# Ends of the expert layers on ScalarE and VectorE alone, and A_log's exponential moved into the projection

## The chip, the cores and the metric

The kernel runs on 1 core of one Trainium2 chip. The metric is the device time of one execution in microseconds (us), and the number compared is the median over several executions.

## What is computed

The input is x, 4 sequences of 512 tokens with 256 channels (2048 rows). Four layers follow, each as x = x + layer(layernorm(x)): attention, an expert layer, a state-space layer, and the same expert layer again.

```
def _L0_ffn_ref(x, W1, b1, W2, b2, W3, b3, Wg, bg):
    gate_weights = softmax(x @ Wg + bg)
    topv, topi = top_k(gate_weights, 2)
    h = gelu(x @ W1[n] + b1[n]); h = gelu(h @ W2[n] + b2[n]); eo = h @ W3[n] + b3[n]
    out = sum over the two chosen experts of topv * eo
...
# state-space layer
dt = softplus(dt + dt_bias)
dA = exp(dt * (-exp(A_log)))
```

Each token thus ends an expert layer with three terms: its own row of x, gate 0 times the output row of its first expert, and gate 1 times that of its second.

## The kernel before, in words

The program is a row of stages, each a block in which all engines run their own instruction stream, with a barrier at its end: constants, layer norm, attention, `ffn_stage` (first expert layer), layer norm "ln2" (`layer_norm_stage`), `ssm_project_stage`, the heads of the state-space layer, `ffn_stage` again. X, [128 partitions, 16 token tiles, 256], stays in SBUF throughout. G is 4 groups of TB = 4 token tiles.

In `ffn_stage` tokens are sorted by expert, gathered in tiles of rows, put through three products with two gelus, and each output row is scattered by GpSimd to `y_rows` in DRAM. When all scatters have landed, the end of the layer begins: SP issues eight loads of 512 KB (L1018), one for each k (0: first expert's rows, 1: second's) and group g, into the tile `back`, in the order of the list BACK: (1,2), (0,0), (1,3), (1,0), (0,1), (1,1), (0,2), (0,3). Each has a semaphore of its own.

- For groups 2 and 3 (BY_POOL) ScalarE multiplies the second rows by their gates in place, four activations a group (L1261), and GpSimd adds the scaled group to X in one tensor_tensor of 128x1024 (L1076).
- VectorE does the rest: for each (k, g) left in that order, four scalar_tensor_tensor of 128x256 (L1449) that multiply a tile's rows by their gate and add them to X, 24 in all. Before the first rows of groups 2 and 3 it waits for GpSimd's sum.
- In the second expert layer only, ScalarE then issues the four stores of the output, 512 KB each (L1267), behind its own scaling in its stream, each when `added` shows that its group is complete.

In ln2, `SsmWeights` runs alongside: SP loads A_log into a_log (L1546) and other small inputs; behind the last activation of the stage ScalarE takes the exponential of a_log (L1565), for which a program puts an activation-table load ahead of it, and VectorE multiplies it by -1 into neg_a (L1560).

`ssm_project_stage` begins with TensorE's products for dt. ScalarE copies them with a bias (L1742, twice), then takes Abs (L1744), Exp (L1746) and Relu (L1747) of 128x1024, and only then the first taps of the convolution (L1755, from PSUM). VectorE adds three more taps to each (L1857, three instructions a block), which frees the bank for TensorE's third block after and lets ScalarE go on to Silu (L1769, with a table load). Between blocks VectorE does the steps of softplus (L1868, L1871, L1874). neg_a is first read much later, by an Exp at L1825.

Of the kernel before, what the change touches and what calls it, by code (L numbers as in the profile page):

```python
# [17 lines left out]
P = 128  # L18
# [858 lines left out]
def ffn_stage(nc, stage, ins, X, split_w, xn_rows, y_rows, row_moves, c, out, split_in):  # L877
# [9 lines left out]
    with ExitStack() as ctx:  # L887
# [63 lines left out]
        weighed, summed = sem("weighed"), sem("summed")  # L951
# [11 lines left out]
        BY_POOL = (2, 3)  # L963
        BACK = [(1, 2), (0, 0), (1, 3), (1, 0), (0, 1), (1, 1), (0, 2), (0, 3)]
# [56 lines left out]
        def _(pool):  # L1021
# [51 lines left out]
            for at, g in enumerate(BY_POOL):  # L1073
                pool.wait_ge(weighed, at + 1)
                x = X[:, g * TB:(g + 1) * TB, :]
                pool.tensor_tensor(x, x, back[:, G + g, :, :], ALU.add).then_inc(summed, 1)  # L1076
# [115 lines left out]
        def _(act):  # L1192
# [65 lines left out]
            for g in BY_POOL:  # L1258
                act.wait_ge(back_loaded[G + g], 16)
                for n in range(TB):  # L1260
                    ins_ = act.activation(back[:, G + g, n, :], back[:, G + g, n, :], ACT.Copy,  # L1261
                                          scale=gate[:, 1, g * TB + n:g * TB + n + 1])
                ins_.then_inc(weighed, 1)
            if out is not None:
                for g in range(G):
                    act.wait_ge(added, (2, 4, 5, 6)[g] * TB)
                    act.dma_start(group_rows(out.rearrange("b s d -> (b s) d"), g),  # L1267
                                  X[:, g * TB:(g + 1) * TB, :]).then_inc(stored, 16)
                act.wait_ge(stored, 16 * G)

        @block.vector
        def _(dve):
# [167 lines left out]

            order = [(k, g) for k, g in BACK if k == 0 or g not in BY_POOL]
            for at, (k, g) in enumerate(order):
                dve.wait_ge(back_loaded[k * G + g], 16)
                if g in BY_POOL:
                    dve.wait_ge(summed, BY_POOL.index(g) + 1)
                elif k:
                    dve.wait_ge(added, TB * (order.index((0, g)) + 1))
                for n in range(TB):
                    dve.scalar_tensor_tensor(X[:, g * TB + n, :], back[:, k * G + g, n, :], gate[:, k, g * TB + n:g * TB + n + 1],  # L1449
                                             X[:, g * TB + n, :], ALU.mult, ALU.add).then_inc(added, 1)  # L1450

# [76 lines left out]
class SsmWeights:  # L1528
# [6 lines left out]
    def __init__(self, t, ins, split, wih, wil, conv_w, conv_b, dt_bias, neg_a, d_col):  # L1535
        self.ins, self.split, self.wih, self.wil, self.conv_w, self.conv_b = ins, split, wih, wil, conv_w, conv_b
        self.dt_bias, self.neg_a, self.d_col = dt_bias, neg_a, d_col
        self.a_log = t.sb("a_log", [P, 1])
        self.loaded, self.exp_ready = t.sem("loaded"), t.sem("exp_ready")

    def sync(self, sp):
        ins, loaded = self.ins, self.loaded
        col = lambda name: ins["L0_attn_b_" + name].unsqueeze(1)
        for half in range(2):
            rows = slice(half * SH, (half + 1) * SH)
            sp.dma_start(self.a_log[rows, :], col("A_log")).then_inc(loaded, 16)  # L1546
# [10 lines left out]
    def vector(self, dve, g):  # L1557
        if g == 4:
            dve.wait_ge(self.exp_ready, 1)
            dve.tensor_scalar(self.neg_a[:, :], self.a_log[:, :], -1.0, None, ALU.mult)  # L1560

    def scalar(self, act, g):
        if g == 4:
            act.wait_ge(self.loaded, 9 * 16)
            act.activation(self.a_log[:, :], self.a_log[:, :], ACT.Exp).then_inc(self.exp_ready, 1)  # L1565
# [5 lines left out]
def ssm_project_stage(nc, XTh, XTl, weights, outs, identf, b_rows):  # L1571
# [9 lines left out]
    with ExitStack() as ctx:  # L1581
# [16 lines left out]
        names = ("cleared dt_psum dt_read dt_exp dt_u dt_done da_done ft_done suffix_done steps hi_done lo_done "  # L1598
# [140 lines left out]
        def _(act):  # L1739
# [6 lines left out]
            act.activation(e, e, ACT.Exp, scale=-1.0).then_inc(s["dt_exp"], 1)  # L1746
            act.activation(u, u, ACT.Relu).then_inc(s["dt_u"], 1)  # L1747
# [52 lines left out]
            for N in range(NB):  # L1800
# [22 lines left out]
                if (b, n) == (2, 0):  # L1823
                    act.wait_ge(s["dt_done"], 1)
                    act.activation(dA, dT, ACT.Exp, scale=neg_a[:, :]).then_inc(s["da_done"], 1)  # L1825
# [19 lines left out]
        def _(dve):  # L1845
# [19 lines left out]
            def softplus():  # L1865

                dve.wait_ge(s["dt_exp"], 2)
                steps(dve.tensor_scalar(dT, e, LOG_SERIES[-1], None, ALU.mult))  # L1868
# [634 lines left out]
```

## Time and profile before

| | |
|---|---|
| median of 3 runs | 1444.76 us (1443.35 to 1449.8) |
| the profiled execution's own time | 1445.6 us |
| its span in the trace | 1443.9 us |
| mean granted TensorE clock | 0.913 |
| PE busy | 1168.8 us (81%) |
| VectorE (DVE) busy | 989.5 us (69%) |
| ScalarE (ACT) busy | 641.4 us (44%) |
| GpSimd (POOL) busy | 609.3 us (42%) |

The span is what the hardware profiler saw from the first to the last instruction; the own time has some 1.7 us around it. Times within the trace count from the span's start. The first expert layer ends near 745 us, ln2 near 764 us, and the second expert layer's end is the end of the program.

### The profile page before, as it was taken

To read this page: it belongs to the slowest core of one execution; us is meant where nothing else is said; L and a number is where in the kernel's file an instruction comes from. 1 tells how busy PE (TensorE), PEld (TensorE's weight loads), DVE (VectorE), ACT (ScalarE), POOL (GpSimd) and SP (SyncE) were. 2 spreads that over 40 slices of the span, in tenths; PEclk is the share of its full clock that TensorE was granted. 3 is DMA by queue.
4 is the path that set the end of the run, shared out by engine and by line. 5 is a ranking of instruction groups with operands and counts; after the bars stand their busy time and mean duration, and the time that the engine had idled before them with its cause. 6 is when DMAs were issued, how large, how long until landed. Compare 5 with 4: busy or idle time off the path is not lost. (4 is left out here: it accounts for less than half of the span.)

```text
span 1443.9 us, 32147 instructions
## 1 busy us (share of the span) xinstructions
PE 1168.8 (81%) x12288; PEld 880.8 (61%) x12288; DVE 989.5 (69%) x2090; ACT 641.4 (44%) x1503; POOL 609.3 (42%) x529
## 2 busy tenths in 40 slices
PE   2789898998874599999817886898999649999991
PEld 1356565665653398898703553665756427989881
DVE  6479798897786555556566957788797574554565
ACT  4367566666564133333436653353333223333341
POOL 0245445545430234334310195688696213333231
PEclk8799999999995699999959997999999758999996
DMA  4645656656533599866240002000000049966725
GB/s 158 154 130 158 171 171 172 167 164 159 145 111 89 187 419 358 283 243 247 63 173 8 19 20 45 16 17 2 2 2 2 30 93 412 410 227 245 257 92 186
DMA packets 98186, 216.83 MB, mean 150 GB/s; under 512 B 28977, under 2 KB 68146, under 8 KB 91890
## 3 DMA queue, kind: packets, MB, share of 16 engines
q1 hardware_dynamic: 88434, 192.22, 41.0%
q0 software_dynamic: 7488, 20.46, 4.2%
q8 instruction: 99, 1.62, 0.5%
q10 hardware_dynamic: 2112, 2.10, 0.4%
q14 instruction: 53, 0.43, 0.1%
HBM read 157.40 MB, written 40.04 MB: 137 GB/s over the span
## 5 line engine op out<-in xcount | busy, mean ns | idle before, releaser
L1233 ACT ACTIVATE ffn_h<-ffn_bank,ffn_b 128x256 f32<-128x256 f32 (+1 forms) x384 | 144.5, 431 | 275.1 <-PE ffn_bank L118 272.9
L1412 DVE CAST ffn_hh<-ffn_h 128x512 f16<-128x512 f32 (+1 forms) x192 | 78.9, 411 | 184.2 <-ACT ffn_h L1233 183.6
L116 PE MATMUL ffn_bank<-ffn_hh,ffn_W 128*128 128x256 f16 (+1 forms) x768 | 180.9, 254 | 8.2 <-DVE ffn_hl L1414 8.1
L1043 POOL DMA_INDIRECT ffn_xs<-xn_rows,ffn_from_rows x78 | 79.0, 1013 | 246.8 <-PE ffn_bank L1128 158.2
L117 PE MATMUL ffn_bank<-ffn_hl,ffn_W 128*128 128x256 f16 (+1 forms) x768 | 180.7, 253 | 0.0
L118 PE MATMUL ffn_bank<-ffn_hh,ffn_W 128*128 128x256 f16 (+1 forms) x768 | 180.6, 253 | 0.0
L644 ACT ACTIVATE att_prob<-att_bank,att_nmax 128x512 f32<-128x512 f32 (+3 forms) x256 | 127.4, 526 | 30.8 <-DVE att_nmax L726 29.5
L733 DVE TENSOR_TENSOR att_ptl<-att_bank,att_pth 128x384 f16<-128x384 f32 (+1 forms) x192 | 114.1, 594 | 34.3 <-ACT att_pth L651 34.3
L651 ACT ACTIVATE att_pth<-att_bank 128x384 f16<-128x384 f32 (+1 forms) x192 | 101.5, 529 | 78.7 <-PE att_bank L591 78.7
L1050 POOL DMA_INDIRECT y_rows<-ffn_y,ffn_to_rows x78 | 77.6, 995 | 127.1 <-DVE ffn_y L1423 83.9
L591 PE MATMUL att_bank<-main_identf,att_prob 128*128 128x128 f32 x640 | 98.8, 279 | 36.9 <-ACT att_prob L644 20.5
L2350 POOL TENSOR_TENSOR ssm_L<-ssm_L,ssml_G 128x512 f32<-128x512 f32 x86 | 110.9, 1305 | 39.9 <-DVE ssm_L L2257 39.9
L836 POOL TENSOR_TENSOR att_rope<-att_turned 128x512 f32<-128x512 f32 x36 | 45.7, 1269 | 192.6 <-DVE att_turned L771 138.2
L2181 ACT ACTIVATE ssmh_windows<-ssml_dtx 64x64 f32<-64x64 f32 x256 | 64.7, 253 | 138.4 <-PE ssm_Y L2080 132.4
L726 DVE TENSOR_REDUCE att_nmax<-att_bank 128x1 f32<-128x512 f32 (+3 forms) x256 | 117.8, 480 | 10.4 <-PE att_bank L581 10.1
L1414 DVE TENSOR_TENSOR ffn_hl<-ffn_h,ffn_hh 128x512 f16<-128x512 f32 (+1 forms) x192 | 116.2, 605 | 6.6
L591 PEld LDWEIGHTS att_bank<-main_identf,att_prob 128*128 128x128 f32 x640 | 71.3, 142 | 57.7 <-ACT att_prob L644 43.8
L2257 DVE TENSOR_TENSOR_SCAN ssm_L<-ssm_bank,ssmh_ident 128x512 f32<-128x512 f32 x86 | 102.2, 1208 | 5.3 <-PE ssm_bank L2068 4.9
L116 PE MATMUL ffn_bank<-ffn_xTh,ffn_W 128*128 128x256 f16 (+1 forms) x384 | 92.1, 257 | 3.4 <-DVE ffn_xTl L1405 3.4
L117 PE MATMUL ffn_bank<-ffn_xTl,ffn_W 128*128 128x256 f16 (+1 forms) x384 | 92.1, 257 | 0.0
L118 PE MATMUL ffn_bank<-ffn_xTh,ffn_W 128*128 128x256 f16 (+1 forms) x384 | 91.9, 256 | 0.0
L116 PE MATMUL ffn_bank<-ffn_W,ffn_hh 128*128 128x256 f16 x312 | 85.3, 273 | 7.2 <-DVE ffn_hl L1414 6.7
(345 smaller groups left out, 3230.5 us busy)
## 6 DMA issues: line engine op xcount, KB each, us to landing
ffn_W<-split_w SPq DMA_DIRECT2D x46, 2048.0 KB, 13.2
att_piece<-in_ffn_w SPq DMA_DIRECT2D x32, 512.0 KB, 5.4
split_w<-att_halves SPq DMA_DIRECT2D x32, 512.0 KB, 4.3
att_Q<-att_pair SPq DMA_DIRECT2D x64, 128.0 KB, 2.4
ffn_back<-y_rows SPq DMA_DIRECT2D x16, 512.0 KB, 7.3
att_KB<-att_krl SPq DMA_DIRECT2D x8, 512.0 KB, 5.5
att_Q<-att_pair SPq DMA_DIRECT2D x64, 64.0 KB, 2.1
xn_rows<-ffn_XN SPq DMA_DIRECT2D x8, 512.0 KB, 2.6
```

What stands on the lines that cost most here:

```text
L116: pe.matmul(out, ah, bh, start=start, stop=False)
L117: pe.matmul(out, ah, bl, start=False, stop=False)
L118: return pe.matmul(out, al, bh, start=False, stop=stop)
L591: ins = pe.transpose(bk[:, j * P:(j + 1) * P], prob[:, g % 2, at + j * P:at + (j + 1) * P], identf[:, :])
L644: ins = act.activation(prob[:, g % 2, p_at[i]:p_at[i] + n], bank[bk][:, at:at + n], ACT.Exp, bias=nmax[:, g % 2, i:i + 1])
L651: act.activation(pth[:, g % 2, at:at + n], bank[5 + (3 * g + c) % 2][:, 0:n], ACT.Copy).then_inc(pT_high, 1)
L726: ins = dve.tensor_reduce(nmax[:, g % 2, i:i + 1], bank[bk][:, at:at + (i + 1) * P], AX.X, ALU.max, negate=True)
L733: dve.tensor_tensor(ptl[:, g % 2, at:at + n], bank[5 + (3 * g + c) % 2][:, 0:n], pth[:, g % 2, at:at + n], ALU.subtract).then_inc(pT_low, 1)
L1233: ins_ = act.activation(h[layer][:, m, 0:n], bank[1 + 2 * layer + u][:, (m % 2) * n:(m % 2 + 1) * n], ACT.Gelu, bias=bias[:, ds(e + m, 1)])
L1414: dve.tensor_tensor(hl[layer][:, half, 0:n], h[layer][:, half, 0:n], hh[layer][:, half, 0:n], ALU.subtract).then_inc(h_low[layer], 1)
L2257: dve.tensor_tensor_scan(slots[p % RING], bank[p % 2][:, :], ident8[:, :], 0.0, ALU.mult, ALU.add).then_inc(scan_done, 1)
L2350: pool.tensor_tensor(slots[p % RING], slots[p % RING], G[:, b, :], ALU.mult).then_inc(mult_done, 1)
```

## The change

At the ends of both expert layers BACK becomes (1,0), (0,0), (1,1), (0,1), (1,2), (0,2), (1,3), (0,3). ScalarE scales the second rows of all four groups. VectorE takes group by group: four scalar_tensor_tensor for the first rows, then one tensor_tensor of 128x1024 that adds the scaled second rows. GpSimd adds nothing. ScalarE's stores wait for (g + 1) * 5 counts of `added`.

A_log is loaded straight into neg_a. ln2 has no exponential and no multiplication by -1. They stand in the projection: the exponential on ScalarE between Exp (L1746) and Relu (L1747), the multiplication on VectorE at the head of softplus, just before L1868; the Exp at L1825 waits for it by the new semaphore a_ready.

```diff
-        BY_POOL = (2, 3)
-        BACK = [(1, 2), (0, 0), (1, 3), (1, 0), (0, 1), (1, 1), (0, 2), (0, 3)]
+        BACK = [(k, g) for g in range(G) for k in (1, 0)]
...
-            for at, g in enumerate(BY_POOL):
-                pool.wait_ge(weighed, at + 1)
-                x = X[:, g * TB:(g + 1) * TB, :]
-                pool.tensor_tensor(x, x, back[:, G + g, :, :], ALU.add).then_inc(summed, 1)
...
-            for g in BY_POOL:
+            for g in range(G):
                 act.wait_ge(back_loaded[G + g], 16)
                 for n in range(TB):
                     ins_ = act.activation(back[:, G + g, n, :], back[:, G + g, n, :], ACT.Copy,
...
-                    act.wait_ge(added, (2, 4, 5, 6)[g] * TB)
+                    act.wait_ge(added, (g + 1) * (TB + 1))
...
-            order = [(k, g) for k, g in BACK if k == 0 or g not in BY_POOL]
-            for at, (k, g) in enumerate(order):
-                dve.wait_ge(back_loaded[k * G + g], 16)
-                if g in BY_POOL:
-                    dve.wait_ge(summed, BY_POOL.index(g) + 1)
-                elif k:
-                    dve.wait_ge(added, TB * (order.index((0, g)) + 1))
+            for g in range(G):
+                dve.wait_ge(back_loaded[g], 16)
                 for n in range(TB):
-                    dve.scalar_tensor_tensor(X[:, g * TB + n, :], back[:, k * G + g, n, :], gate[:, k, g * TB + n:g * TB + n + 1],
+                    dve.scalar_tensor_tensor(X[:, g * TB + n, :], back[:, g, n, :], gate[:, 0, g * TB + n:g * TB + n + 1],
                                              X[:, g * TB + n, :], ALU.mult, ALU.add).then_inc(added, 1)
+                dve.wait_ge(weighed, g + 1)
+                dve.wait_ge(added, g * (TB + 1) + TB)
+                x = X[:, g * TB:(g + 1) * TB, :]
+                dve.tensor_tensor(x, x, back[:, G + g, :, :], ALU.add).then_inc(added, 1)
...
     def vector(self, dve, g):
-        if g == 4:
-            dve.wait_ge(self.exp_ready, 1)
-            dve.tensor_scalar(self.neg_a[:, :], self.a_log[:, :], -1.0, None, ALU.mult)
+        pass
 
     def scalar(self, act, g):
-        if g == 4:
-            act.wait_ge(self.loaded, 9 * 16)
-            act.activation(self.a_log[:, :], self.a_log[:, :], ACT.Exp).then_inc(self.exp_ready, 1)
+        pass
...
             act.activation(e, e, ACT.Exp, scale=-1.0).then_inc(s["dt_exp"], 1)
+            act.activation(neg_a[:, :], neg_a[:, :], ACT.Exp).then_inc(s["a_exp"], 1)
             act.activation(u, u, ACT.Relu).then_inc(s["dt_u"], 1)
...
                     act.wait_ge(s["dt_done"], 1)
+                    act.wait_ge(s["a_ready"], 1)
                     act.activation(dA, dT, ACT.Exp, scale=neg_a[:, :]).then_inc(s["da_done"], 1)
...
                 dve.wait_ge(s["dt_exp"], 2)
+                dve.wait_ge(s["a_exp"], 1)
+                dve.tensor_scalar(neg_a[:, :], neg_a[:, :], -1.0, None, ALU.mult).then_inc(s["a_ready"], 1)
                 steps(dve.tensor_scalar(dT, e, LOG_SERIES[-1], None, ALU.mult))
```

## Rows read from the trace of the kernel before

**Rows 1.** Chain that ended last, end of the second expert layer: start, us, what

```profile
1421.17 4.52 DMA ffn_back<-y_rows
...
1429.64 5.25 DVE main_X L1449 x8
...
1436.27 3.56 DVE main_X L1449 x9
```

**Rows 2.** Timeline at the two ends: start, us, engine, line, out<-in, [idle before]

```profile
730.69 14.15 DVE L1449 SCALAR_TENSOR_TENSOR main_X<-ffn_back,ffn_gate,main_X 128x256 f32<-128x256 f32 x24 [10.10 <-DMA ffn_back<-y_rows]
...
1425.72 14.11 DVE L1449 SCALAR_TENSOR_TENSOR main_X<-ffn_back,ffn_gate,main_X 128x256 f32<-128x256 f32 x24 [8.39 <-DMA ffn_back<-y_rows]
```

**Rows 3.** Timeline, one instruction of VectorE and one of GpSimd

```profile
1426.12 2.63 DVE L1449 SCALAR_TENSOR_TENSOR main_X<-ffn_back,ffn_gate,main_X 128x256 f32<-128x256 f32 x1
...
1426.12 2.34 POOL L1076 TENSOR_TENSOR main_X<-main_X,ffn_back 128x1024 f32<-128x1024 f32 x1 [7.55 <-ACT ffn_back L1261]
```

**Rows 4.** All instructions on ffn_back: duration ns min/median/max, first and last start

```profile
L1449 DVE SCALAR_TENSOR_TENSOR main_X<-ffn_back,ffn_gate,main_X x48: 471/476/2629, 730.7 to 1439.4; 128x256 f32<-128x256 f32 x48
...
L1261 ACT ACTIVATE ffn_back<-ffn_back,ffn_gate x16: 492/494/508, 729.4 to 1428.9; 128x256 f32<-128x256 f32 x16
L1076 POOL TENSOR_TENSOR main_X<-main_X,ffn_back x4: 2334/2456/2607, 731.2 to 1429.5; 128x1024 f32<-128x1024 f32 x4
```

**Rows 5.** VectorE's tensor_tensor of 128x1024, both inputs in SBUF, by shape

```profile
L1874 DVE TENSOR_TENSOR proj_late<-proj_late,ssml_zs 128x1024 f32<-128x1024 f32 x1 | 1.2, 1215 | 0.0
```

**Rows 6.** Single loads of ffn_back: issue, then landing; first end's 4th, 8th, second's 7th

```profile
L1018 SPq DMA_DIRECT2D ffn_back<-y_rows x1: 432/432/432, 727.1 to 727.1; - x1
DMA to landing us min/median/max: 7.0/7.0/7.0
...
L1018 SPq DMA_DIRECT2D ffn_back<-y_rows x1: 446/446/446, 729.1 to 729.1; - x1
DMA to landing us min/median/max: 10.1/10.1/10.1
...
L1018 SPq DMA_DIRECT2D ffn_back<-y_rows x1: 446/446/446, 1423.9 to 1423.9; - x1
DMA to landing us min/median/max: 8.9/8.9/8.9
```

**Rows 7.** Output stores: last issue, landing, and ScalarE's queue in 1410 to 1444

```profile
1439.86 0.38 ACTq L1267 DMA_DIRECT2D out<-main_X  x1
...
out<-main_X ACTq DMA_DIRECT2D x4, 512.0 KB, 3.0
...
q10 hardware_dynamic: 2112, 2.10, 18.4%
```

**Rows 8.** Timeline, end of ln2 and start of the projection

```profile
760.48 2.74 DVE L205 TENSOR_TENSOR ssmi_XTl<-ln_bank,ssmi_XTh 128x512 f16<-128x512 f32 x4 [1.15 <-ACT ssmi_XTh L241]
...
762.51 1.28 ACT L1565 ACT_TABLE_LOAD   x1
763.80 0.20 ACT L1565 ACTIVATE ln_a_log<-ln_a_log 128x1 f32<-128x1 f32 x1
764.04 0.15 DVE L1560 TENSOR_SCALAR ssmi_neg_a<-ln_a_log 128x1 f32<-128x1 f32 x1 [0.82 <-ACT ln_a_log L1565]
...
773.93 1.06 ACT L1746 ACTIVATE ssml_zs<-ssml_zs 128x1024 f32<-128x1024 f32 x1
...
775.84 1.83 ACT L1755 ACTIVATE proj_taps<-proj_bank,ssmi_conv_w 128x512 f32<-128x512 f32 x3
776.63 2.32 DVE L1857 SCALAR_TENSOR_TENSOR proj_taps<-proj_bank,ssmi_conv_w,proj_taps 128x511 f32<-128x511 f32 x3 [10.43 <-ACT proj_taps L1755]
...
779.01 0.39 PE L116 MATMUL proj_bank<-ssmi_XTh,ssmi_wih 128*128 128x512 f16 x1 [0.79 <-DVE proj_taps L1857]
```

**Rows 9.** Windows: length, busy us of PE, PEld, DVE, ACT, POOL, clock, DMA share, GB/s

```profile
776.00:800.00 24.00, 18.82 (x155) 9.14 (x154) 22.66 (x28) 14.86 (x24) 0.00 (x0) 1.00 0.04 12
...
764.00:765.00 1.00, 0.00 (x0) 0.00 (x0) 0.15 (x1) 0.01 (x1) 0.18 (x1) 1.00 0.00 0
765.00:766.00 1.00, 0.84 (x3) 0.33 (x4) 0.71 (x1) 0.00 (x0) 0.37 (x1) 0.50 0.00 0
...
769.00:770.00 1.00, 1.00 (x7) 0.41 (x6) 0.00 (x0) 0.47 (x1) 0.00 (x0) 1.00 0.00 0
```

More of the change, by code:

```diff
@@ L950, in ffn_stage @@
         back_loaded = [sem(f"back_loaded{i}") for i in range(TOPK * G)]
-        weighed, summed = sem("weighed"), sem("summed")
+        weighed = sem("weighed")
         added, stored = sem("added"), sem("stored")
@@ L1537, in __init__ @@
         self.dt_bias, self.neg_a, self.d_col = dt_bias, neg_a, d_col
-        self.a_log = t.sb("a_log", [P, 1])
-        self.loaded, self.exp_ready = t.sem("loaded"), t.sem("exp_ready")
+        self.loaded = t.sem("loaded")
     def sync(self, sp):
@@ L1545, in sync @@
             rows = slice(half * SH, (half + 1) * SH)
-            sp.dma_start(self.a_log[rows, :], col("A_log")).then_inc(loaded, 16)
+            sp.dma_start(self.neg_a[rows, :], col("A_log")).then_inc(loaded, 16)
             sp.dma_start(self.dt_bias[rows, :], col("dt_bias")).then_inc(loaded, 16)
@@ L1597, in ssm_project_stage @@
         bank = t.banks()
-        names = ("cleared dt_psum dt_read dt_exp dt_u dt_done da_done ft_done suffix_done steps hi_done lo_done "
+        names = ("cleared a_exp a_ready dt_psum dt_read dt_exp dt_u dt_done da_done ft_done suffix_done steps hi_done lo_done "
                  "conv_psum copied tapped silu z_psum z_done xt_psum xt_done b_psum b_done g_psum g_done "
```

## The prediction

> **What bounds the kernel now.** Every stage ends in a barrier, so I read the change where its stages end, not in the busy shares. First the chain that ended last [rows 1]: at the end of the second expert layer it runs from the loads of the expert rows into VectorE's multiply-adds (L1449) and stays there to 1436.27 + 3.56 = 1439.83. Eight of them take 5.25 us in the middle and nine take 3.56 us later, 0.396 us each: the stretch in the middle holds something more. The timeline shows the whole: 24 of them from 730.69 to 744.84 at the first end, from 1425.72 to 1439.83 at the second [rows 2], where 24 x 0.396 are 9.5 us. The rest, some 4.6 us an end, is found among single instructions: one multiply-add takes 2.63 us over the very time in which GpSimd's add takes 2.34 us [rows 3], and the extremes, 471 ns against 2629 ns at a median of 476 ns, with two GpSimd adds an end, say the same [rows 4]. So VectorE bounds both ends, and loses about 2.1 us to each GpSimd add.
>
> For the second part I read the timeline across the barrier behind ln2 [rows 8]. VectorE's last real work ends at 760.48 + 2.74 = 763.22; a table load, a one-column exponential and VectorE's product end at 764.19, and the stage ends on them. In the projection ScalarE goes from Exp (773.93) through Relu to the first tap (775.84) without a pause; VectorE waits for it, and TensorE then for VectorE (its first wait ends at 779.01). From 776 to 800 VectorE is busy 22.66 of 24 us [rows 9]. So a delay of the first tap delays the stage.
>
> **First end, part by part.** Removed: two GpSimd adds and with them two stalls, and 8 of 24 multiply-adds. Added on VectorE: four adds of 128x1024. The very form stands in the trace at 1.215 us [rows 5]. A group costs 3 x 0.396 + 0.476 = 1.66 us for the first rows, 1.22 us for the add, and I put 0.1 us for its two waits: of 14.11 us at the second end, 9.50 for 24 multiply-adds and 2 x (2.63 - 0.48) = 4.30 for stalls leave 0.3 us over all changes from block to block, 0.04 us each, which is the lower end; the upper is 0.4 us. That is 2.98 us, four groups 11.9 us, from 730.69 to 742.6. But now loads 2, 4, 6 and 8 gate the groups. Load 4 lands at 727.1 + 7.0 = 734.1 [rows 6], group 0 ends at 733.7: 0.4 us of waiting. Load 8 lands at 729.1 + 10.1 = 739.2, when VectorE still has group 2 in hand (it reaches group 3 at about 740.1). The end is 743.0 against 744.84: **-1.8 us**. Bounds: load 8 plus one group's work gives 742.1 (-2.7 us); 0.3 us more waiting a group gives 744.2 (-0.6 us). ScalarE's extra eight scalings cost nothing: a group takes it at most 4 x 0.494 = 2.0 us [rows 4] from the odd load, and the even load lands some 1.27 us later ((739.2 - 734.1) / 4) with 1.66 us of multiply-adds in front of the add. If that cover went, VectorE would wait for ScalarE by the difference, a few tenths. The reordered loads are the same eight through the same queue; SP is moved past nothing.
>
> **Second end.** The same on VectorE: 1425.72 + 11.9 + 0.4 = 1438.0 against 1439.83. Here stores follow. Their waits stand behind ScalarE's scaling of group 3, which needs load 7, landed at 1423.9 + 8.9 = 1432.8 [rows 6]; so no store goes out before 1434.5, when groups 0 and 1 have long been added and group 2 nearly has. That keeps the stores off the last load. It also sends three together. ScalarE's queue took 18.4% of a 34 us window for four stores, 1.56 us each with all 16 engines, and a store alone lands after 3.0 us [rows 7]. Before, they went one by one and the last, issued at 1439.86, landed at 1442.9. Now four times 1.56 us run from about 1434.5 + (3.0 - 1.56) = 1435.9 to 1442.2, though VectorE was done at 1438.0. So the end gains **-0.7 us**; the ends of this cost are -1.9 us (transfers overlap and the last store lands 3.0 us after its issue) and 0 (stores in a row slower than one by one). I take the queue, because its time a store is from the row of the same transfer.
>
> **Exponential of A_log.** ln2 ends at 763.22 instead of 764.19: -0.97 us. The table load doesn't vanish: the layer norm's square root leaves another table, and the first exponential is now Exp at L1746, so the load of 1.28 us lies between Abs and Exp, where ScalarE has no gap. The small exponential takes 0.20 us there [rows 8]. The first tap thus comes 1.28 + 0.20 - 0.1 (an estimate of the overlap of two activations; 773.93 + 1.06 + 1.06 would be past the first tap's 775.84 by that) later in its stage, 0.97 us earlier by the stage: +0.4 us. VectorE's product, 0.15 us, now stands in its busiest stretch, +0.1 us. The new waits find their signals long given: a_exp comes before Relu, the reader of neg_a is tens of us later. Sum **+0.5 us**. Bounds: -0.8 us if the load is put ahead of the copies, where ScalarE sits idle; +0.8 us if nothing overlaps.
>
> The row shows that an activation starts 0.01 us behind the load before it [rows 8]. The Trainium skill, page "ScalarE: Activation LUTs", section "What ACT_TABLE_LOAD costs", gives 1283 ns for the load and about 1380 ns more for a drain at each switch. The trace agrees on the load, 1.28 us, and shows nothing of the drain. By the page the part would be +1.9 us and the whole -0.6 us.
>
> **Sum.** -1.8 + 0.5 - 0.7 = -2.0 us. Against the profiled execution that is 1445.6 - 2.0 = 1443.6 us; the median of the runs lies 0.8 us below that execution, so I say 1444.8 - 2.0 = **1442.8 us**, 0.14% less. A measurement of this kernel can tell about 0.5% (7 us) from no change: I forecast no change that can be told.
>
> **Rivals.**
> 1. *The clock comes back later* (slower). The granted clock fell to half (1.2 GHz) at 765, just as TensorE restarted after its pause, and was full again before 769; at half it does 3 to 4 products a us, at full 6 to 7 [rows 9]. The projection now starts 2.8 us earlier after another pause. Each us longer at half costs 0.5 us while TensorE leads, so from 4 us more on it eats the whole gain; lasting over both dt products and the first convolution blocks, 5.2 us more, it gives 1442.8 + 2.6 = 1445.4. For: the fall comes of a pause, and pauses are moved. Against: the pause gets shorter. Chance 0.15.
> 2. *Clock kept and stores overlapped* (more gain). The pause before the projection shrinks by 1 us, and at 764 the clock was still full [rows 9]; if it doesn't fall, about 1.7 us of the first product are saved, and overlapping stores save 1.2 us more: 1439.9. Chance 0.15.
> 3. *The change doesn't do what it says*: the moved load is placed ahead of the two copies, in ScalarE's idle time. Then the part gives -0.8 and the whole -3.3 us: 1441.5. Against: other loads stand right before the function that needs them, as at L1565. Chance 0.1.
> 4. *The switch costs more than its row*, a pause of 1.4 us between Abs and Exp that at ln2's end lay elsewhere: 1444.2. Against: the 0.01 us of rows 8. Chance 0.05. (The drain that the Trainium skill states on "ScalarE: Activation LUTs" would act as this rival.)
> 5. *VectorE isn't freed*: the 2.6 us multiply-adds come from the loads' traffic, not from GpSimd. They would stay, and an end would take 12.3 + 4.3 = 16.6 us instead of 14.1: 1444.8 + 2 x 2.5 + 0.5 = 1450.3. Against: exactly one long instruction for each GpSimd add, of its length. Chance 0.03.
> The forecast has 0.52.
>
> **Range and chances.** The forecast and rivals 1 to 4, 0.97, lie within 1439.9 to 1445.4. The runs of before spread from 1.4 below to 5.0 us above their median, which no case explains, and part of it will be in the median of after. So 1438.5 to 1447.5. Over 0.5% faster means under 1437.5: 0.05, only rival 2 with a low draw. Over 0.5% slower, above 1452: 0.03, from rival 5 or rival 1 with a high draw. The rest, 0.92, is within 0.5%.
>
> **What would show it.** VectorE's 16 multiply-adds and 4 adds at each end with no instruction over 1.3 us, lasting about 12.3 us; GpSimd idle there; first end near 743.0; three stores issued within 1.3 us from about 1433.2 (1434.5, and all before it 1.3 us earlier), the last landing later than 3 us after its issue; ln2 without a table load, one of 1.28 us at L1746, the first tap 0.4 us later against the end of the first expert layer's barrier than now. Wrong would be: a long multiply-add without GpSimd; adds well over 1.22 us; first rows waiting for loads by more than 0.5 us; a time that moves by more than 7 us.

## The result, and the profile after

The changed kernel took 1442.93 us in the median of 12 runs (1439.42 to 1448.9), the kernel before, run beside it, 1448.87 us (12 runs, 1443.35 to 1452.3). The ratio is 0.9968, with a 95% interval of 0.9953 to 0.9983. The same program was compared twice more on other occasions: 0.9963 [0.9944, 0.9982] and 0.9977 [0.9957, 0.9997]. The mean of the three is 0.9969, some 4.5 us: less than before, by less than the 0.5% named in the prediction, and more than the 2.0 us forecast. All three intervals lie below 1, so the difference can be told from no change; the prediction had put the limit of what can be told at 0.5%, and these intervals reach 0.15 to 0.2% to either side. That the median came within 0.2 us of 1442.8 is no merit: the kernel before had medians of 1448.87, 1446.92, 1443.0, 1442.87 and 1442.53 us in the comparisons of this study.

The profiled execution took 1443.96 us, with a span of 1442.2 us against 1443.9. First the second expert layer's end in the timeline of the kernel after (start, us, engine, line, operation, what it waited for).

```profile
1425.90 1.67 DVE L1439 SCALAR_TENSOR_TENSOR main_X<-ffn_back,ffn_gate,main_X 128x256 f32<-128x256 f32 x4 [8.39 <-DMA ffn_back<-y_rows]
1427.67 1.23 DVE L1444 TENSOR_TENSOR main_X<-main_X,ffn_back 128x1024 f32<-128x1024 f32 x1
...
1429.41 1.67 DVE L1439 SCALAR_TENSOR_TENSOR main_X<-ffn_back,ffn_gate,main_X 128x256 f32<-128x256 f32 x4 [0.51 <-DMA ffn_back<-y_rows]
...
1433.23 0.51 ACT L1256 ACTIVATE ffn_back<-ffn_back,ffn_gate 128x256 f32<-128x256 f32 x1 [0.84 <-DMA ffn_back<-y_rows]
1433.24 0.43 ACTq L1262 DMA_DIRECT2D out<-main_X  x1
...
1437.01 1.22 DVE L1444 TENSOR_TENSOR main_X<-main_X,ffn_back 128x1024 f32<-128x1024 f32 x1
```

And all instructions of the kernel after on the loaded rows (duration min/median/max in ns), the answer to [rows 4].

```profile
L1439 DVE SCALAR_TENSOR_TENSOR main_X<-ffn_back,ffn_gate,main_X x32: 476/479/485, 732.7 to 1436.4; 128x256 f32<-128x256 f32 x32
...
L1444 DVE TENSOR_TENSOR main_X<-main_X,ffn_back x8: 1224/1225/1225, 734.5 to 1437.0; 128x1024 f32<-128x1024 f32 x8
```

No multiply-add is over 485 ns where the longest was 2629 ns; the adds cost 1.225 us. VectorE's first end ran from 732.70 to 744.44, 11.74 us instead of 14.15 [rows 2]; the second ended at 1438.23, after 12.33 us, with a wait of 0.51 us for a load in it. The first store goes out at 1433.24, while ScalarE still has nearly all of group 3 to scale: the scalings run from 1433.23 to 1434.94, so here the store, which stands behind them in the stream, did not wait for them to be done.

The start of the projection in the kernel after, to be read against [rows 8]. TensorE's first product and ScalarE's second copy of the kernel before, which those rows leave out, come first.

```profile
765.15 0.59 PE L116 MATMUL proj_bank<-ssmi_XTh,ssmi_wih 128*128 128x512 f16 x1 [3.30 <-PEq L77]
772.12 0.69 ACT L1742 ACTIVATE ssml_zs<-proj_bank,ssmi_dt_bias 128x512 f32<-128x512 f32 x1 [1.90 <-PE proj_bank L118]
```

```profile
760.07 2.81 DVE L205 TENSOR_TENSOR ssmi_XTl<-ln_bank,ssmi_XTh 128x512 f16<-128x512 f32 x4 [1.15 <-ACT ssmi_XTh L241]
...
763.86 0.38 PE L116 MATMUL proj_bank<-ssmi_XTh,ssmi_wih 128*128 128x512 f16 x1 [2.33 <-PEq L77]
...
770.92 0.69 ACT L1732 ACTIVATE ssml_zs<-proj_bank,ssmi_dt_bias 128x512 f32<-128x512 f32 x1 [1.90 <-PE proj_bank L118]
771.64 1.06 ACT L1734 ACTIVATE ssml_zs<-ssml_zs 128x1024 f32<-128x1024 f32 x1
772.72 1.28 ACT L1736 ACT_TABLE_LOAD   x1
774.01 1.06 ACT L1736 ACTIVATE ssml_zs<-ssml_zs 128x1024 f32<-128x1024 f32 x1
774.98 0.18 ACT L1737 ACTIVATE ssmi_neg_a<-ssmi_neg_a 128x1 f32<-128x1 f32 x1
775.07 1.04 ACT L1738 ACTIVATE ssml_zs<-ssml_zs 128x1024 f32<-128x1024 f32 x1
776.01 1.82 ACT L1746 ACTIVATE proj_taps<-proj_bank,ssmi_conv_w 128x512 f32<-128x512 f32 x3
776.80 2.31 DVE L1849 SCALAR_TENSOR_TENSOR proj_taps<-proj_bank,ssmi_conv_w,proj_taps 128x511 f32<-128x511 f32 x3 [11.90 <-ACT proj_taps L1746]
```

ln2 ends on its last real work, and TensorE starts 0.98 us behind it instead of 1.93. The load moved between Abs and Exp: from the second copy to the first tap it is 5.09 us instead of 3.72.

To compare executions I use three stretches of their profiles, given in the table in us, that leave out what went before them. A: VectorE's first multiply-add of the first end to its last instruction there. B: from that instant to VectorE's first sum of taps in the projection. C: VectorE's first multiply-add of the second end to the end of the span. The last two columns are the start of A and the ratio to before.

| kernel | A | B | C | sum | A starts | ratio [95%] |
|---|---|---|---|---|---|---|
| before | 14.15 | 31.79 | 18.18 | 64.12 | 730.69 | |
| after | 11.74 | 32.36 | 16.30 | 60.40 | 732.70 | 0.9968 [0.9953, 0.9983] |
| after_again | 11.74 | 33.65 | 15.71 | 61.10 | 729.77 | 0.9963 [0.9944, 0.9982] |
| after_third | 12.50 | 32.38 | 16.41 | 61.29 | 723.88 | 0.9977 [0.9957, 0.9997] |
| ends_only | 12.47 | 32.39 | 16.37 | 61.23 | 734.02 | 0.9957 [0.9938, 0.9976] |
| alog_only | 14.18 | 32.32 | 17.97 | 64.47 | 732.28 | 1.0006 [0.999, 1.0022] |
| early_exp | 12.15 | 32.04 | 16.00 | 60.19 | 730.13 | 0.9955 [0.9934, 0.9975] |
| pool_add | 15.02 | 32.34 | 19.01 | 66.37 | 731.43 | 1.0029 [1.0013, 1.0046] |
| pool_memset | 11.75 | 34.73 | 15.76 | 62.24 | 730.47 | 0.9994 [0.9972, 1.0015] |
| stores_between | 11.75 | 32.32 | 15.94 | 60.01 | 726.80 | 0.9974 [0.9954, 0.9993] |
| add_on_vector | 14.26 | 32.01 | 18.23 | 64.50 | 730.25 | 0.999 [0.9971, 1.0009] |
| vector_alone | 13.67 | 33.67 | 17.53 | 64.87 | 723.20 | 1.0001 [0.9982, 1.002] |
| early_exp_stores | 11.94 | 31.92 | 16.72 | 60.58 | 729.72 | 0.9965 [0.9945, 0.9985] |
| order_with_pool | 13.55 | 36.75 | 18.80 | 69.10 | 730.79 | 1.0021 [1.0002, 1.0039] |

The same instructions lead up to A in all of them, and yet it starts anywhere from 723.20 to 734.02. The part between B and C, again the same instructions, took from 645.4 to 650.7 us. One execution's span therefore says nothing about 2 or 4 us; the stretches do, and for the kernel before they rest on one profile (the ends of alog_only, which are the same, have 14.18 and 17.97 us).

### The profile page after: what moved, and what is told of

It reads as the page before. It is cut to its first block and busy times, and to the rows that moved or that the text cites. A ratio compares the mean times of both kernels' runs of the same rounds, so it can differ in the third digit from the quotient of the medians.

```text
span 1442.2 us, 32153 instructions
## 1 busy us (share of the span) xinstructions
PE 1169.6 (81%) x12288; PEld 881.9 (61%) x12288; DVE 985.1 (68%) x2082; ACT 647.3 (45%) x1519; POOL 599.3 (42%) x525
```

## The experiments

### The changed kernel again

after_again and after_third are the changed kernel without an edit, each beside other kernels and the same runs of before.

> The changed kernel once more, beside the three parts of it, so that all stand against the same runs of the kernel before. Theory (the steps as the changed kernel's own trace shows them: first end 11.7 us of VectorE instead of 14.1, second end 1.9 us shorter to the end of the span, first tap of the projection 0.6 us later behind the first end): 3.7 us less than before. Rival (the measured 4 to 6 us come in part from TensorE's granted clock, which happened to be low for longer in the runs of before): a ratio that differs from the first comparison by 0.1% or more, with the same steps in the trace.

> The changed kernel beside the three above. Theory: first end 11.7 to 12.0 us, second 15.7 to 16.3 us, 5.1 us from the second copy to the first tap; time 3.7 us below before, within the interval. Rival (something outside the three places of the edit gives the rest of the measured 4 to 6 us): a ratio of 0.9965 or less a third time.

Neither rival came out as it was put: 0.9963 is 0.05% from the first ratio, not 0.1%, and the third ratio is 0.9977, not 0.9965 or less. The clock does differ between the profiles, though: B of after_again is 1.3 us longer than in the first profile with the same steps, and the next section shows why. In after_third the first end took 12.50 us and the second 16.41, both above the ranges named, since VectorE waited 0.66 and 0.55 us for loads; the 5.09 us to the first tap came as expected. The sums of the three stretches are 3.0 and 2.8 us below before, 3.7 in the first profile: 3.2 us on average, where timing says 4.5 us with an interval of 2 to 3 us either way for each comparison. The two agree within what was measured; whether the last 1.3 us are real stays open. I found no place outside the three stretches that would give them.

### The two parts alone

ends_only takes the change of `ffn_stage` and leaves A_log in ln2; alog_only does the reverse.

```diff
# ends_only, against the changed kernel
+        if g == 4:
+            act.wait_ge(self.loaded, 9 * 16)
+            act.activation(self.a_log[:, :], self.a_log[:, :], ACT.Exp).then_inc(self.exp_ready, 1)
...
-            act.activation(neg_a[:, :], neg_a[:, :], ACT.Exp).then_inc(s["a_exp"], 1)
...
# alog_only, against the kernel before: the reverse of these lines, ffn_stage untouched
```

> The ends of both expert layers as changed, A_log's exponential back in the layer norm. Theory: all of the gain and the 0.6 us that the moved exponential costs: 4.3 us less than before, ratio 0.9970; in the trace the first end takes 11.7 us of VectorE, and from its last instruction to the first tap's sum 31.8 us as before. Rival (the moved exponential gives a good part of the gain): 2 us or less below before.

> A_log's exponential moved, the ends as before. Theory: +0.6 us, ratio 1.0004, the table load of 1.28 us between Abs and Exp in the projection, layer norm 1 us shorter, 32.4 us from VectorE's last multiply-add of the first end to the first tap's sum instead of 31.8. Rival (the move is a gain): -1 us or less, with 30.8 us for that stretch.

ends_only has the whole gain, 0.9957; alog_only has none, 1.0006, and its A and C are those of before. In ends_only the first end took 12.47 us, not the 11.7 expected: VectorE waited 0.64 us for a load. B can't be read without the clock, so I split it. TensorE starts 1.93 us behind ln2's last VectorE work in ends_only as before, 1.13 us in alog_only. From the second copy to the first tap it is 3.71 us in ends_only and 5.09 in alog_only. The rows of alog_only:

```profile
773.62 1.06 ACT L1739 ACTIVATE ssml_zs<-ssml_zs 128x1024 f32<-128x1024 f32 x1
774.69 1.28 ACT L1741 ACT_TABLE_LOAD   x1
775.99 1.06 ACT L1741 ACTIVATE ssml_zs<-ssml_zs 128x1024 f32<-128x1024 f32 x1
776.95 0.19 ACT L1742 ACTIVATE ssmi_neg_a<-ssmi_neg_a 128x1 f32<-128x1 f32 x1
```

So the move takes 0.8 to 0.95 us out and puts 1.38 us in: a loss of 0.4 to 0.6 us, in the size of the theory, too small to be told by time.

B as a whole says the same once TensorE's clock is taken out of it. The granted clock was at half (1.2 GHz) for 3 to 6 us between TensorE's start in the projection and VectorE's first sum of taps. Over that stretch, in before, after and after_again (length, busy times of PE, PEld, DVE, ACT and POOL, clock, DMA share, GB/s):

```profile
765.15:776.63 11.48, 10.69 (x42) 4.41 (x43) 0.91 (x1) 5.13 (x7) 0.22 (x1) 0.86 0.01 1
763.86:776.80 12.94, 12.16 (x48) 4.94 (x48) 0.91 (x2) 6.50 (x9) 0.21 (x1) 0.87 0.00 0
761.15:775.16 14.01, 13.23 (x48) 5.17 (x48) 0.89 (x2) 6.50 (x9) 0.06 (x1) 0.80 0.01 1
```

A stretch of length L with the mean clock c was at half for 2 x (1 - c) x L. I take half of that time off B, an estimate by which TensorE's work costs double at half (the table uses the clock unrounded):

| A_log's exponential | us at half clock in B | B | B less half of them |
|---|---|---|---|
| in ln2: before, ends_only, add_on_vector | 3.3, 4.2, 3.4 | 31.79, 32.39, 32.01 | 30.2, 30.3, 30.3 |
| between Exp and Relu: after, after_again, after_third, alog_only | 3.4, 5.6, 3.1, 3.4 | 32.36, 33.65, 32.38, 32.32 | 30.7, 30.9, 30.9, 30.6 |
| the same: pool_add, stores_between, vector_alone | 3.3, 3.2, 6.0 | 32.34, 32.32, 33.67 | 30.7, 30.7, 30.7 |
| ahead of the copies: early_exp, early_exp_stores | 5.1, 5.3 | 32.04, 31.92 | 29.5, 29.3 |

Within each place of the exponential the values now lie within 0.3 us, where B itself was spread over up to 1.35 us. The 0.6 us by which ends_only's B exceeds the 31.8 expected is for the most part such time, 0.5 us. The move costs 0.5 us, and the place ahead of the copies takes 0.9 us off before.

### The exponential where ScalarE is idle

```diff
         def _(act):
+            act.activation(neg_a[:, :], neg_a[:, :], ACT.Exp).then_inc(s["a_exp"], 1)
             for r in range(PAIRS):
...
-            act.activation(neg_a[:, :], neg_a[:, :], ACT.Exp).then_inc(s["a_exp"], 1)
...
             link(dve.memset(starts[:, :], 0.0))
+            dve.wait_ge(s["a_exp"], 1)
+            dve.tensor_scalar(neg_a[:, :], neg_a[:, :], -1.0, None, ALU.mult).then_inc(s["a_ready"], 1)
...
-                dve.wait_ge(s["a_exp"], 1)
-                dve.tensor_scalar(neg_a[:, :], neg_a[:, :], -1.0, None, ALU.mult).then_inc(s["a_ready"], 1)
```

> The changed kernel with the exponential of A_log as ScalarE's first instruction of the projection, ahead of its wait for TensorE, and the product with -1 behind VectorE's memset. Theory: the table load falls into ScalarE's idle 6 us and the chain from Abs to the first tap loses 1.28 + 0.09 us, VectorE's first stretch 0.1 us: 1.4 us less than the changed kernel, 5.1 us less than before, ratio 0.9965; in the trace 30.9 us from VectorE's last instruction of the first end to the first tap's sum. Rival (the first tap is bound by TensorE's product, not by ScalarE's chain): no less than the changed kernel.

Timeline of early_exp:

```profile
761.68 1.28 ACT L1730 ACT_TABLE_LOAD   x1 [1.61 <-PEq L77]
762.97 0.20 ACT L1730 ACTIVATE ssmi_neg_a<-ssmi_neg_a 128x1 f32<-128x1 f32 x1
...
767.32 0.69 ACT L1733 ACTIVATE ssml_zs<-proj_bank,ssmi_dt_bias 128x512 f32<-128x512 f32 x1 [4.14 <-PE proj_bank L118]
769.90 0.69 ACT L1733 ACTIVATE ssml_zs<-proj_bank,ssmi_dt_bias 128x512 f32<-128x512 f32 x1 [1.90 <-PE proj_bank L118]
...
773.62 0.67 ACT L1746 ACTIVATE proj_taps<-proj_bank,ssmi_conv_w 128x512 f32<-128x512 f32 x1
```

The load lies in the wait for TensorE, and the chain from the second copy to the first tap is 3.72 us instead of 5.09: the 1.37 us of the theory to the hundredth. B itself is 32.04, not the 30.9 expected, because TensorE's first product took 5.30 us to ScalarE's copy where it took 4.38 before and 4.47 after. That is the clock, at half for 5.1 us here: by the table above, B without it is 1.3 us shorter than in the changed kernel. The median was 1439.86 us, beside 1441.69 for the changed kernel in the same comparison; their intervals overlap widely.

### Does GpSimd hold VectorE up, and with what?

The changed kernel gets useless work on GpSimd at each end, on the tiles h[0] and h[1]: in pool_add two adds, in pool_memset two times three memsets. The output is not touched by it.

```diff
...
+            for at in range(2):
+                pool.wait_ge(weighed, at + 1)
+                pool.tensor_tensor(h[0][:, :, :], h[1][:, :, :], h[1][:, :, :], ALU.add).then_inc(cleared, 1)
...
# pool_memset: pool.memset(h[0][:, :, :], 0.0), three times, in its place
```

> The changed kernel with two GpSimd adds of 128x1024 at each end on tiles that nobody reads any more (h), when the first and the second group are scaled. No data passes from them to VectorE or back. Theory (a GpSimd add holds up VectorE's instructions with two inputs in SBUF for its whole length): one VectorE instruction of about 2.6 us, or an add of about 3.4 us, for each, and each end 2.1 to 2.3 us longer a GpSimd add, 4.3 us in all. Rival (VectorE was late in the kernel before because of the order and the wait for the sums): no VectorE instruction over 1.3 us and ends of 11.7 us.

> The same with three GpSimd memsets of 128x1024 in place of each add, which write as much and read nothing. Theory (what blocks is GpSimd's reading of SBUF): VectorE's multiply-adds and adds keep 0.48 and 1.22 us and the ends 11.7 us. Rival (any GpSimd instruction on SBUF blocks): VectorE instructions lengthened by up to the memset's 0.9 us, and ends 4 us longer or so.

Second end in pool_add, then in pool_memset:

```profile
1426.12 2.10 POOL L1076 TENSOR_TENSOR ffn_h<-ffn_h 128x1024 f32<-128x1024 f32 x1 [7.64 <-ACT ffn_back L1262]
1429.00 1.22 DVE L1450 TENSOR_TENSOR main_X<-main_X,ffn_back 128x1024 f32<-128x1024 f32 x1
1429.52 2.46 POOL L1076 TENSOR_TENSOR ffn_h<-ffn_h 128x1024 f32<-128x1024 f32 x1 [1.29 <-ACT ffn_back L1262]
1430.15 2.11 DVE L1445 SCALAR_TENSOR_TENSOR main_X<-ffn_back,ffn_gate,main_X 128x256 f32<-128x256 f32 x1
```

```profile
1425.14 6.00 POOL L1077 MEMSET ffn_h<- 128x1024 f32 x6 [7.79 <-ACT ffn_back L1263]
1426.31 1.23 DVE L1451 TENSOR_TENSOR main_X<-main_X,ffn_back 128x1024 f32<-128x1024 f32 x1
1427.45 1.67 DVE L1446 SCALAR_TENSOR_TENSOR main_X<-ffn_back,ffn_gate,main_X 128x256 f32<-128x256 f32 x4
```

With no data passing between them, each GpSimd add lengthens one multiply-add to 2.1 us, and A goes from 11.74 to 15.02 us. Six memsets, 6 us of GpSimd without a break in VectorE's busiest time, do nothing: A is 11.75, and no multiply-add is over 485 ns. So GpSimd's add blocks an instruction of VectorE with two SBUF inputs, and a memset, which reads nothing, doesn't. The Trainium skill has a rule for it in "SBUF — State Buffer", section "SBUF: two separate sides": the shared pair of ports is an exclusive lock held for the whole instruction, and a two-input VectorE instruction meets it only against a GpSimd operation that reads SBUF. Both halves agree with these two runs.

Two places elsewhere in the kernel before show where a rule from these runs alone would go wrong. VectorE's cast of 128x512 (L1412), with one input, takes at most 0.53 us without a GpSimd tensor_tensor beside it, and took 1.32, 1.65 and 1.84 us beside a tensor_tensor of GpSimd with two inputs. And a two-input multiply-add of 128x1024 (L1871) kept its 1.215 us twice beside a tensor_scalar of GpSimd that had begun first and reads one tile of SBUF and a column of factors (L1907). The rows of one case each:

```profile
656.06 1.65 DVE L1412 CAST ffn_hh<-ffn_h 128x512 f16<-128x512 f32 x1 [2.80 <-ACT ffn_h L1233]
655.83 1.59 POOL L1519 TENSOR_TENSOR ffn_wi_lo<-ffn_wi,ffn_wi_hi 128x736 f16<-128x736 f32 x1
...
806.22 1.22 DVE L1871 SCALAR_TENSOR_TENSOR proj_late<-proj_late,ssml_zs 128x1024 f32<-128x1024 f32 x1
805.63 3.23 POOL L1907 TENSOR_SCALAR ssml_skip<-ssml_skip,ssml_d_col 128x512 f32<-128x512 f32 x2 [40.26 <-PE proj_bank L1670]
```

The other traces show the same of both (the second case costs at most 0.17 us there). So it isn't every GpSimd instruction that reads, as the Trainium skill's rule and my theory have it, and it isn't two-input instructions of VectorE alone. Nor is it everything: the sums of taps (L1857), with one input in PSUM, kept 0.75 us beside a GpSimd tensor_tensor of 1.89 us (L1917). What these traces show is that GpSimd's two-input tensor_tensor blocks VectorE's instructions on SBUF alone; why its one-input instruction doesn't stays open.

The size was off by a quarter: 3.3 us an end, not 4.3. The second GpSimd add began at 1429.52 during VectorE's add and took 2.46 us, and the one at the first end took 2.85, where the shortest took 1.99: I read the difference as GpSimd waiting for VectorE, which no run separates. A lengthened multiply-add is 2.12 us long, 1.64 more than its own 0.48. By time pool_add is 0.6% above the changed kernel's ratios, some 9 us, of which the stretches show 5 to 6; the rest stays open. pool_memset's ratio, 0.9994, shows none of the changed kernel's gain although both its ends are as short; its B is long, as said below.

### The stores between the scalings

```diff
+            def store(g):
+                act.wait_ge(added, (g + 1) * (TB + 1))
...
             for g in range(G):
                 act.wait_ge(back_loaded[G + g], 16)
...
                 ins_.then_inc(weighed, 1)
+                if out is not None and g:
+                    store(g - 1)
+            if out is not None:
+                store(G - 1)
```

> The changed kernel with the output's stores between ScalarE's scalings (group g - 1 stored behind the scaling of group g) instead of behind them all. Theory: the first store goes out at about 1429.8 and moves while loads 6 to 8 are under way, each store's 1.56 us of all transfer engines lies in front of them, the last load lands 1.5 to 3 us later, and the end comes 0.5 to 2 us later than in the changed kernel. Rival (stores and loads pass one another, and what binds the end is the bunch of stores behind the scaling): the end comes as early or earlier, with the last load in its place.

```profile
1420.90 0.42 ACTq L1255 DMA_DIRECT2D out<-main_X  x1
...
1426.72 3.48 ACTq L1255 DMA_DIRECT2D out<-main_X  x2
1426.78 1.67 DVE L1443 SCALAR_TENSOR_TENSOR main_X<-ffn_back,ffn_gate,main_X 128x256 f32<-128x256 f32 x4
```

The theory was wrong here. The first store went out 3.04 us behind VectorE's start (1417.86), amid the loads, and VectorE reached its last group at 1426.78 0.18 us later than it would have without a wait (1.14 us behind the start of its add at 1425.46). C is 15.94 us, between the 15.71 and 16.41 of the changed kernel. The loads were in fact delayed: the first store took 7.1 us from issue to landing, where one took 3.0 before, and loads 7 and 8 landed 1.8 and 2.0 us behind the load ahead of them instead of 1.3. The last thus landed 1.2 us late, at 1426.76, but VectorE had group 2 in hand until 1426.60, so it cost 0.18 us: the delay was in the theory, the cover wasn't. Neither place for the stores is worth anything against the other: the last store, issued right behind VectorE's last add and landed 3 us later, sets the end in both.

### What of the ends' gain is the order, what is GpSimd's absence?

add_on_vector is the kernel before with GpSimd's two adds an end given to VectorE; order_with_pool is the changed kernel with those two adds given back to GpSimd; vector_alone is the changed kernel with all second rows on VectorE as multiply-adds.

```diff
# add_on_vector, against the kernel before
                 if g in BY_POOL:
-                    dve.wait_ge(summed, BY_POOL.index(g) + 1)
+                    dve.wait_ge(weighed, BY_POOL.index(g) + 1)
+                    x = X[:, g * TB:(g + 1) * TB, :]
+                    dve.tensor_tensor(x, x, back[:, G + g, :, :], ALU.add).then_inc(summed, 1)
+                    dve.wait_ge(summed, BY_POOL.index(g) + 1)
# order_with_pool, against the changed kernel
+            for g in (2, 3):
+                pool.wait_ge(weighed, g + 1)
+                x = X[:, g * TB:(g + 1) * TB, :]
+                pool.tensor_tensor(x, x, back[:, G + g, :, :], ALU.add).then_inc(summed, 1)
...
# vector_alone, against the changed kernel
-                dve.tensor_tensor(x, x, back[:, G + g, :, :], ALU.add).then_inc(added, 1)
+                for n in range(TB):
+                    dve.scalar_tensor_tensor(X[:, g * TB + n, :], back[:, G + g, n, :], gate[:, 1, g * TB + n:g * TB + n + 1],
+                                             X[:, g * TB + n, :], ALU.mult, ALU.add).then_inc(added, 1)
```

> The kernel before with one edit: the two adds of 128x1024 that GpSimd made at each end are VectorE's, in the same place of its order; loads, scalings, stores and A_log stay. Theory (GpSimd's add holds VectorE up for its whole length, so VectorE loses 2.1 us for work that costs it 1.2 us): an end takes 24 x 0.396 + 2 x 1.22 + 0.5 = 12.4 us of VectorE instead of 14.1, 3.4 us in all, ratio 0.9976. Rival (the gain needs the new order and the shorter work on VectorE): 14 us or more an end, since VectorE has two instructions more.

> The changed kernel with GpSimd's adds back for groups 2 and 3 (ahead of VectorE's multiply-adds, which wait for the sum), in the new order of loads. The question is what of the gain the order alone gives. Theory (both are needed: without GpSimd's adds the old order waits 1.9 us for a load, and with them the new order is held up): GpSimd's second sum can't be there before load 7 plus 1.7 us of scaling plus 2.3 us, 11.2 us behind VectorE's start, and four multiply-adds follow, so an end takes 12.9 to 13.7 us, with one VectorE instruction an add lengthened to 2 us or more. Rival (the order alone is the gain): 11.7 to 12.5 us.

> The changed kernel with all second rows multiplied and added by VectorE, 32 multiply-adds an end, ScalarE and GpSimd doing nothing there. Theory: 32 x 0.396 = 12.7 us and 8 changes of block at 0.04 to 0.1 us, 13.0 to 13.4 us an end: 1.3 to 1.6 us more than the changed kernel an end, and still 0.8 to 1.1 us less than the kernel before with three engines at work. Rival (the help of two engines was worth something before): longer than 14.1 us.

First end of add_on_vector:

```profile
730.25 1.67 DVE L1448 SCALAR_TENSOR_TENSOR main_X<-ffn_back,ffn_gate,main_X 128x256 f32<-128x256 f32 x4 [10.16 <-DMA ffn_back<-y_rows]
...
733.80 5.03 DVE L1448 SCALAR_TENSOR_TENSOR main_X<-ffn_back,ffn_gate,main_X 128x256 f32<-128x256 f32 x12 [1.88 <-DMA ffn_back<-y_rows]
738.75 1.22 DVE L1443 TENSOR_TENSOR main_X<-main_X,ffn_back 128x1024 f32<-128x1024 f32 x1
```

The stall is gone and the end takes 14.26 us all the same: my 12.4 failed. Behind its first block VectorE now stands 1.88 us for the load of (1,0), the fourth in the old order, and does 1.25 us more work for each add. In the kernel before this wait lay beneath GpSimd's first stall. In the new order the fourth load is (0,1), and the gap before it is filled with the first group's add. Of the 2.5 us from add_on_vector to the changed kernel the wait is 1.9; the other 0.6 or so is that VectorE has one add in place of four multiply-adds in groups 0 and 1.

First end of order_with_pool:

```profile
736.50 2.40 POOL L1075 TENSOR_TENSOR main_X<-main_X,ffn_back 128x1024 f32<-128x1024 f32 x1 [12.96 <-ACT ffn_back L1260]
739.00 5.34 DVE L1445 SCALAR_TENSOR_TENSOR main_X<-ffn_back,ffn_gate,main_X 128x256 f32<-128x256 f32 x8 [2.30 <-POOL main_X L1075]
739.06 2.62 POOL L1075 TENSOR_TENSOR main_X<-main_X,ffn_back 128x1024 f32<-128x1024 f32 x1 [0.16 <-ACT ffn_back L1260]
```

The new order with GpSimd takes 13.55 us, as expected: VectorE waits 2.30 us for the first sum and is held up by the second. Its second end took VectorE 14.08 us, above the 13.7. Of the 2.4 us that A gained, neither edit alone gives more than 0.6; each uncovers what the other removes. vector_alone took 13.67 and 13.52 us of VectorE at its two ends, a little over my 13.0 to 13.4, since each second block begins with a wait for VectorE's own first block and costs 1.77 us instead of 1.59. It shows that at 32 multiply-adds one engine alone was no slower in this stretch than three together before; by time it stands where the kernel before does, 1.0001.

order_with_pool and pool_memset hold something that I can't explain: ln2 started 4.77 and 2.39 us behind VectorE's last instruction of the first end, 1.0 us in all other profiles. It makes their B long: without it, and with the clock taken out as above, they have 30.7 and 30.9 us like the changed kernel. Whether it comes in every execution, and so explains their ratios, one profile each can't show.

### Both additions together

early_exp_stores joins the edits of early_exp and stores_between.

> The changed kernel with A_log's exponential as the projection's first instruction on ScalarE and the stores between the scalings. Theory: the parts of the two runs add: 3.7 us from Identity's second copy to the first tap instead of 5.1, second end 15.7 to 16.3 us to the end of the span, 1.4 us less than the changed kernel, ratio to before 0.996. Rival (stores early in the end delay the last loads after all, and the run before was favoured by an early start): second end 17 us or more.

The second copy to the first tap takes 3.72 us; C is 16.72, above the 16.3 expected and under the rival's 17, for VectorE waited longer for loads (12.71 us to its last add). Its median was 1437.44 us, beside 1438.43 for the changed kernel and 1443.0 for the kernel before. That is the right way and the right size, 1 us for 1.4, and not told apart by its interval. I count only the 1.37 us of the moved load as shown.

## Why the prediction was right, and where not

- *VectorE bounds both ends and is held up by GpSimd's adds*: right, and shown by pool_add and pool_memset. Rival 5 fell: no multiply-add of the changed kernel is over 485 ns under the same loads.
- *The first end, -1.8 us*: -2.4 in the first profile, -2.4 and -1.65 in the other two. The terms were right (1.67 and 1.225 us, 2.92 us a group with no wait, my 2.98). What varied is the waiting for loads, which I put at 0.4 us: nothing, nothing, and 0.7 us. By my own list a wait of over 0.5 us for the first rows would be a sign of being wrong; it was reached in three profiles (0.51 in the first, 0.66 and 0.55 in after_third, 0.64 in ends_only), so the bound on this term was too narrow. Left out altogether was why the order is part of it.
- *The second end, -0.7 us*: this is the term that was mis-sized. C fell by 1.88, 2.47 and 1.77 us. VectorE's part was right (12.33 us, my 12.3). I had let three stores wait for ScalarE's last scaling to finish, 1434.5, and had four of them queue to 1442.2. The first went out at 1433.24, the second at 1433.71 and the third, which waited for VectorE's add of group 2, at 1435.35 (2.1 us from the first to the third, not the 1.3 of my list), and their transfers ran from 1434.2 on instead of 1435.9. These windows of the kernel after (length, busy times, clock, DMA share, GB/s), behind the landing of the loads, show the stores moving well before the last is issued at 1438.3:

```profile
1434.00:1435.00 1.00, 0.00 (x0) 0.00 (x0) 0.91 (x1) 0.94 (x3) 0.00 (x0) 0.50 0.79 267
1435.00:1436.00 1.00, 0.00 (x0) 0.00 (x0) 1.00 (x3) 0.00 (x0) 0.00 (x0) 0.50 1.01 339
...
1438.00:1439.00 1.00, 0.00 (x0) 0.00 (x0) 0.23 (x1) 0.00 (x0) 0.00 (x0) 0.50 0.82 283
...
1441.00:1442.00 1.00, 0.00 (x0) 0.00 (x0) 0.00 (x0) 0.00 (x0) 0.00 (x0) 0.50 0.00 0
```

  So the three were through as the last one's data had to move, and from VectorE's last add to the span's end it is 4.0 us, as before. The lower bound that I named for this cost, -1.9, was the value to take.
- *A_log's exponential, +0.5 us*: right in size and place. 0.95 us out (forecast 0.97), 1.37 in (1.38), 0.14 us of VectorE's product; 0.5 us by B with the clock taken out. Rival 3 fell: the load stands between Abs and Exp in all three profiles of the changed kernel. Rival 4 fell: from the load's end to Exp it is 0.01 us, and the section "What ACT_TABLE_LOAD costs" of the Trainium skill's "ScalarE: Activation LUTs", with its drain of 1380 ns, isn't borne out in this chain: the load begins 0.02 us behind Abs's end, and the chain grew by 1.37 us in all.
- *Rivals 1 and 2, the clock*: neither as I drew it. In every profile the clock was at half at TensorE's start in the projection or fell to it within 0.9 us, and the copy of the first product came 4.28 to 5.32 us behind TensorE's start for the same instructions. In the kernel after the clock was at 0.87 in the microsecond from 764, at 0.50 to 768 and full from 769, much as before [rows 9]. My reading of those rows was too short: in the kernel before the clock had been at half since 724.0, rose at 761.6 for 3.4 us in which TensorE was nearly idle (busy for 0.16 of 3.2 us), and fell again at 765.0. In six of the 14 profiles, after_again and after_third among them, it was at half from the first end into the projection without a rise, so the full clock at 764 was no state that rival 2 could count on. The price that rival 1 gave was about right, 0.5 us for each us at half: it is what brings the values of B together, and after_again, 5.6 us at half, paid 1.1 us more for it than the kernel after. But with 3.1 to 5.6 us in the three profiles of the changed kernel and 3.3 to 4.2 in the three with A_log in ln2, the edit moved it neither way that can be told from chance.
- *The sum, -2.0 us*: -3.2 us by the stretches on average (A -2.2, B +1.0 with the clock's chance in it, C -2.0), -3.7 with the clock taken out of B (+0.5), -4.5 by the timings. The forecast of no change beyond 0.5% held; its size was too small, by the stores' term above all (-2.0 for -0.7), and by what of the timings stays open.

## What to carry to other kernels

A GpSimd add of two SBUF tiles given away to relieve VectorE cost VectorE more than doing the add itself: 2.1 us in the kernel before and 1.64 in pool_add, against 1.22, while VectorE worked on two SBUF inputs. A memset cost nothing. When such a stall is removed, ask what it covered: here a load's landing, so that only the new order of loads turned it into time. And a table load belongs in front of a wait: moved from a stage's end into a chain without gaps it was a loss of 0.5 us, put ahead of the chain it was free, 0.9 us less than before.

## What was not expected of the hardware

- ScalarE's sequencer issued a store at 1433.24, in the same moment in which the first of four activations ahead of it in the stream began.
- GpSimd's add seems to be held up by VectorE as well: 2.85 us for an add whose shortest was 1.99. And a one-input cast of VectorE was held up by GpSimd, 1.65 us for 0.43, while a one-input instruction of GpSimd held up a two-input one of VectorE by 0.17 us at most.
- With stores amid the loads, both together moved 407 GB/s from 1420 to 1423 and 315 from 1423 to 1427, the last load landed 1.2 us late, and VectorE lost 0.18 us to it.
- The time at which the first expert layer's end began varied by 10.8 us between profiles of kernels with the same instructions before it, and the medians of the kernel before between comparisons by 6.3 us; the four later comparisons ran on four different chips.
